# Moving the expert-weight preparation out of the attention loop of a fused patch-embed, attention and mixture-of-experts kernel

## The reference, cut to what matters

```python
h = concatenate([tok(x), txt], axis=1)                # [32, 164, 192]
h = h + attn(layernorm(h))                            # keys, values, gate of batch 0 alone
# attn: fw = 0.95*fw + 0.1*g0*(k0 outer v0); retrieved = q @ fw; x + retrieved @ w_out.T
h = h + ffn(layernorm(h))
# ffn: xn = rms_norm(x); probs = softmax(xn @ router_w.T); top 2 of 8 experts
#      y = sum over the two of probs[e] * (silu(xn @ gate_w[e].T) * (xn @ up_w[e].T)) @ down_w[e].T
#      result y + x
```

## Time and profile before

| what | us |
|---|---|
| median of three runs | 677.99 |
| the profiled execution, its own time | 683.48 |
| its span, first to last instruction | 681.7 |
| PE busy in the span | 543.7 |
| DVE busy | 406.0 |
| ACT busy | 300.6 |
| POOL busy | 198.3 |

### The profile page before, as it was taken

How to read it: one execution, slowest core, us unless ns; L and a number is a source line. 1 busy time by engine, 2 the same in 40 slices (tenths; PEclk the granted TensorE clock), 3 DMA queues, 4 the chain that set the end, 5 groups by cost and what they waited for, 6 DMA issues and landing times.

```text
span 681.7 us, 13237 instructions
## 1 busy us (share of the span) xinstructions
PE 543.7 (80%) x3330; PEld 504.9 (74%) x3331; DVE 406.0 (60%) x1343; ACT 300.6 (44%) x696; POOL 198.3 (29%) x293
## 2 busy tenths in 40 slices
PE   0079989997699999997019999999999999999300
PEld 0067688997497788886019999999999999999300
DVE  4590717666314789999715656565665656565297
ACT  0035991223523677876314444444544444444100
POOL 0001510000000267777702333333333333333300
PEclk9999997999579999998559999999999999999855
DMA  9999600000951022222222322222222222222398
GB/s 201 236 173 187 120 0 1 7 1 0 225 159 36 22 73 74 82 78 81 78 77 52 82 68 80 69 80 69 69 80 72 77 68 81 68 80 61 107 373 259
DMA packets 85235, 64.87 MB, mean 95 GB/s; under 512 B 42500, under 2 KB 81896, under 8 KB 84824
## 3 DMA queue, kind: packets, MB, share of 16 engines
q1 hardware_dynamic: 67160, 39.93, 26.4%
q0 software_dynamic: 8208, 16.95, 6.9%
q10 hardware_dynamic: 9840, 7.67, 3.9%
HBM read 42.61 MB, written 21.86 MB: 95 GB/s over the span
## 4 chain that ended last, share of the span: by engine, by line
PE 65%; DVE 15%; ACT 8%; DMA 6%; issue 3%; SPq 2%; ACTq 1%; POOL 0%; POOLq 0%; DVEq 0%
PE pair L736 9%; PE bank L931 5%; PE bank L927 5%; PE bank L928 4%; PE bank L930 4%; PE bank L929 4%; PE bank L938 4%; DVE hres L1334 4%; ACT sqjunk L463 4%; PE pair L947 4%; PE bank L947 4%; DMA bet<-in_L_tok_ln_beta 3%; PE pair L916 3%; PE pair L806 3%; PE bank L687 3%
## 5 line engine op out<-in xcount | busy, mean ns | idle before, releaser
L648 POOL DMA_INDIRECT disp<-xf,posu x82 | 79.7, 972 | 166.6 <-DVE posu L1212 142.0
L660 POOL DMA_INDIRECT ydram<-ysb,dnow x89 | 87.3, 981 | 69.4 <-POOL dnow L657 67.1
L1310 DVE TENSOR_TENSOR hh<-sg,bank 128x384 f32<-128x384 f32 x89 | 49.3, 554 | 84.0 <-ACT sg L601 84.0
L601 ACT ACTIVATE sg<-bank 128x384 f32<-128x384 f32 x89 | 43.7, 491 | 110.9 <-PE bank L931 110.9
L736 PE MATMUL pair<-wcT,imgT 128*128 128x193 f32 x432 | 74.7, 335 | 3.3 <-DVE tmp L1048 3.3
L736 PEld LDWEIGHTS pair<-wcT,imgT 128*128 128x128 f32 x432 | 73.7, 196 | 3.5 <-issue 3.5
L927 PE MATMUL bank<-wa,xh 128*128 x178 | 67.5, 379 | 0.0
L931 PE MATMUL bank<-wa,xl 128*128 x178 | 60.0, 337 | 0.0
L928 PE MATMUL bank<-wa,xh 128*128 x178 | 60.0, 337 | 0.0
L929 PE MATMUL bank<-wa,xl 128*128 x178 | 59.8, 336 | 0.0
L930 PE MATMUL bank<-wa,xh 128*128 x178 | 59.7, 335 | 0.0
(11 more groups left out here) (229 smaller groups left out, 1258.0 us busy)
## 6 DMA issues: line engine op xcount, KB each, us to landing
xs<-disp SPq DMA_DIRECT2D x89, 96.0 KB, 2.0
img<-in_x SPq DMA_DIRECT2D x12, 392.0 KB, 8.3
yall<-ydram SPq DMA_DIRECT2D x5, 768.0 KB, 13.9
yall<-ydram ACTq DMA_DIRECT2D x5, 768.0 KB, 15.0
hres<-in_txt SPq DMA_DIRECT2D x4, 768.0 KB, 13.2
xs<-disp SPq DMA_DIRECT2D x89, 33.5 KB, 1.9
wraw<-in_L_tok_W SPq DMA_DIRECT2D x1, 2880.0 KB, 17.0
raw_gu<-in_L_ffn_gate_w SPq DMA_DIRECT2D x7, 288.0 KB, 10.7
```

Source lines behind the costliest of these rows:

```text
L648: pool.indirect_dma_start(disp, bass.IndirectOffsetOnAxis(ap=posu[c % XBUF][:, 2 * j + k:2 * j + k + 1], axis=0), xfd[c % XBUF][:, j, :], None
L660: pool.indirect_dma_start(ydram, bass.IndirectOffsetOnAxis(ap=dnow[b][:], axis=0), ysb[b][:], None).then_inc(s_ys[b], 16)
L1310: v.tensor_tensor(hh[o][:], sg[o][:], bank[2 * o + 1][:, 0:DE], ALU.mult).then_inc(s_hh, 1)
```

## The change

All weight units leave the attention loop and run behind it, over four banks (2, 3, 0, 1) instead of two. On PE units 0 to 3 stand right behind the last chunk, ahead of the last ranks and of the counts, and the other 40 behind the counts. On ACT all 44 stand behind the last `add_norm2`. On DVE all 44 stand behind the table.

In a chunk, PE now takes the ranks of the chunk before right after the first `past`, and goes tile by tile. DVE takes `picks(c)` ahead of `stats_2(c)` and `mask(c+1)`, and `places(c)` in the same chunk, ahead of `scale2(c)`; the row numbers are written by one instruction instead of two, and the two small copies into `xf` move from DVE to ACT, into `norm2`. SP's fills wait for the counts (`s_cnt`) alone, not for the table, and the fill that needs no count goes first. The exponentials and weights move behind the expert loop: on DVE behind its last slot, on ACT behind its loads of `yall`.

```diff
@@ -333,6 +332,13 @@
             k = n - NE * FC // 2
             return None if k < 0 else (k // 4, k // 2 % 2, k % 2)
 
+        def unit_bank(n):
+            return (2, 3, 0, 1)[n % 4]
+
+        def unit_done(n):
+
+            return max((k + 1 for k in range(n) if unit_bank(k) == unit_bank(n)), default=0)
+
         def load_results(eng, t):
 
             n = min(GROUP, TILES - t)
@@ -384,12 +390,13 @@
             for which, w in enumerate((gate_w, up_w)):
                 sp.dma_start(raw_last[:, which], w[NE - 1].rearrange("(c f) d -> f c d", f=P)).then_inc(s_raw7, 16)
 
-            sp.wait_ge(s_tab, 1)
+            sp.dma_start(disp[NE * REGION:NE * REGION + P, :], zrow[:]).then_inc(s_zf, 16)
+            sp.wait_ge(s_cnt, 1)
             for e in range(NE):
                 n = sp.value_load(cti[0:1, 1, e:e + 1], min_val=0, max_val=TILES * P)
                 sp.dma_start(disp[bass.ds(n + e * REGION, P), :], zrow[:]).then_inc(s_zf, 16)
-            sp.dma_start(disp[NE * REGION:NE * REGION + P, :], zrow[:]).then_inc(s_zf, 16)
             sp.wait_ge(s_zf, 16 * (NE + 1))
+            sp.wait_ge(s_tab, 1)
 
             for p in range(XBUF):
                 for j in range(4):
@@ -540,9 +547,14 @@
 
             def norm2(c):
                 act.wait_ge(s_s2, c + 1)
-                for j in range(nt(c)):
-                    if c >= XBUF:
-                        act.wait_ge(s_scat[c % XBUF][j], scattered(c))
+                n, x = nt(c), c % XBUF
+                if c >= XBUF:
+                    for j in range(n):
+                        act.wait_ge(s_scat[x][j], scattered(c))
+                nc.scalar.copy(xfd[x][:, 0:n, D + 1:DROW],
+                               cst[:, C_DEST + 4 * c:C_DEST + 4 * c + n].unsqueeze(2).to_broadcast([P, n, 2]))
+                nc.scalar.copy(xfd[x][:, 0:n, D], idxf[:, 8 * c:8 * c + 2 * n].rearrange("p (j k) -> p j k", k=2)[:, :, 0])
+                for j in range(n):
                     nc.scalar.activation(xfd[c % XBUF][:, j, 0:D], hres3[:, 4 * c + j, :], ACT.Identity,
                                          scale=rs[:, c, 1, j:j + 1], bias=bb[:, c, 1, j:j + 1]).then_inc(s_xf, 1)
 
@@ -570,26 +582,22 @@
             for c in range(CHUNKS):
                 if c + 1 < CHUNKS:
                     xT_out(c + 1, 0)
-                high(4 * c)
-                high(4 * c + 1)
                 if c + 1 < CHUNKS and nt(c + 1) > 2:
                     xT_out(c + 1, 1)
                 if c:
                     norm2(c - 1)
                 if c + 1 < CHUNKS:
                     state_out(c + 1)
-                high(4 * c + 2)
                 if c + 2 < CHUNKS:
                     rows(c + 2)
                 if c:
                     add_norm2(c - 1)
                 std2(c)
-                high(4 * c + 3)
             norm2(CHUNKS - 1)
             add_norm2(CHUNKS - 1)
-
-            act.wait_ge(s_w, 1)
-            nc.scalar.activation(top8[:, 0:8 * TILES], top8[:, 0:8 * TILES], ACT.Exp).then_inc(s_exp, 1)
+            for n in range(UNITS):
+                high(n)
+
 
             def step(k, b, parts="xsht"):
 
@@ -614,6 +622,8 @@
                 act.wait_ge(s_ys[b], 16 * ((SLOTS + 1 - b) // 2))
             for g in range(GROUP, TILES, 2 * GROUP):
                 load_results(act, g)
+            act.wait_ge(s_w, 1)
+            nc.scalar.activation(top8[:, 0:8 * TILES], top8[:, 0:8 * TILES], ACT.Exp).then_inc(s_exp, 1)
             store_results(act, 1)
 
         @block.gpsimd
@@ -829,9 +839,9 @@
                 if n == NE * FC // 2:
                     pe.wait_ge(s_rawg, 16 * 2 * (NE - 1))
                     pe.wait_ge(s_raw7, 32)
-                if n >= 2:
-                    pe.wait_ge(s_lo, n - 1)
-                b = bank[2 + n % 2]
+                if unit_done(n):
+                    pe.wait_ge(s_lo, unit_done(n))
+                b = bank[unit_bank(n)]
                 if unit(n) is None:
                     for kk in range(2):
                         e, c = (2 * n + kk) // FC, (2 * n + kk) % FC
@@ -853,7 +863,6 @@
             for c in range(CHUNKS):
                 if c + 1 < CHUNKS:
                     turn(c + 1, 0)
-                expert(4 * c)
                 pe.wait_ge(s_ns, c + 1)
                 pe.wait_ge(s_rows, 2 * c + 2)
                 if c:
@@ -861,40 +870,39 @@
                 if c >= 2:
                     pe.wait_ge(s_pos, c - 1)
                 past(c, 0)
-                if nt(c) > 2:
-                    past(c, 2)
+                if c:
+                    ranks(c - 1)
                 pe.wait_ge(s_sm, c + 1)
                 last = present(c, 0)
                 if nt(c) > 2:
-                    present(c, 2)
-                else:
-                    last.then_inc(s_o, 1)
-                expert(4 * c + 1)
+                    past(c, 1)
+                    last = present(c, 1)
+                last.then_inc(s_o, 1)
                 if c + 1 < CHUNKS and nt(c + 1) > 2:
                     turn(c + 1, 1)
                 if nt(c) > 2:
-                    past(c, 1)
-                    present(c, 1).then_inc(s_o, 1)
                     if c:
-                        ranks(c - 1)
+                        pe.wait_ge(s_pos, c)
+                    past(c, 2)
+                    present(c, 2)
                     past(c, 3)
                     present(c, 3).then_inc(s_o, 1)
-                else:
-                    ranks(c - 1)
                 if c + 1 < CHUNKS:
                     state(c)
-                expert(4 * c + 2)
                 if c + 2 < CHUNKS:
                     rows(c + 2)
                 if c + 1 < CHUNKS:
                     scores(c + 1)
-                expert(4 * c + 3)
-
+
+            for n in range(4):
+                expert(n)
             pe.wait_ge(s_pos, CHUNKS - 1)
             ranks(CHUNKS - 1)
             pe.wait_ge(s_pos, CHUNKS)
             pe.matmul(bank[6][:, RK + 64:RK + 64 + NE], onesb[:], ecs[:, :, nt(CHUNKS - 1)], start=True, stop=True
                       ).then_inc(s_cread, 1)
+            for n in range(4, UNITS):
+                expert(n)
 
             pe.wait_ge(s_lo, UNITS)
             pe.wait_ge(s_tab, 1)
@@ -1201,15 +1209,11 @@
                                         bank[6][:, RK:RK + NE * n].rearrange("p (e j) -> p j e", e=NE).unsqueeze(2)
                                         .to_broadcast([P, n, 2, NE]), ALU.mult))
                 st.link(v.tensor_reduce(rk, ohm[:, 0:16 * n].rearrange("p (a e) -> p a e", e=NE), AX.X, ALU.add))
-                st.link(v.scalar_tensor_tensor(out=posf[:, 0:2 * n], in0=fi, scalar=float(REGION), in1=rk,
-                                               op0=ALU.mult, op1=ALU.add))
                 if c >= XBUF:
                     for j in range(n):
                         v.wait_ge(s_scat[x][j], scattered(c))
-                st.mark(v.tensor_copy(xfd[x][:, 0:n, D + 1:DROW],
-                                      cst[:, C_DEST + 4 * c:C_DEST + 4 * c + n].unsqueeze(2).to_broadcast([P, n, 2])))
-                st.mark(v.tensor_copy(xfd[x][:, 0:n, D], fi.rearrange("p (j k) -> p j k", k=2)[:, :, 0]))
-                v.tensor_copy(posu[x][:, 0:2 * n], posf[:, 0:2 * n]).then_inc(s_pos, 1)
+                v.scalar_tensor_tensor(out=posu[x][:, 0:2 * n], in0=fi, scalar=float(REGION), in1=rk,
+                                       op0=ALU.mult, op1=ALU.add).then_inc(s_pos, 1)
 
             def scale2(c):
                 n = nt(c)
@@ -1236,31 +1240,22 @@
                 ins.then_inc(s_lo, 1)
 
             mask(0)
-            low(0)
-            low(1)
             for c in range(CHUNKS):
                 residual(c)
                 sums(c)
-                if c:
-                    places(c - 1)
+                picks(c)
                 stats_2(c)
-                low(4 * c + 2)
                 if c + 1 < CHUNKS:
                     mask(c + 1)
-                low(4 * c + 3)
-                picks(c)
-                if c + 1 < CHUNKS:
-                    low(4 * c + 4)
+                places(c)
                 scale2(c)
-                if c + 1 < CHUNKS:
-                    low(4 * c + 5)
-            places(CHUNKS - 1)
 
             v.wait_ge(s_cread, 1)
             cnt, til, cum, fst, one = (ct[:, k, :] for k in range(5))
             st.mark(v.memset(one, 1.0))
             st.mark(v.tensor_scalar(cnt, bank[6][:, RK + 64:RK + 64 + NE], float(P - 1), None, ALU.add))
-            st.link(v.tensor_copy(cti[:, 1, :], bank[6][:, RK + 64:RK + 64 + NE]))
+            v.tensor_copy(cti[:, 1, :], bank[6][:, RK + 64:RK + 64 + NE]).then_inc(s_cnt, 1)
+            st.wait()
             st.link(v.tensor_copy(cti[:, 0, :], cnt))
             st.link(v.tensor_scalar(cti[:, 0, :], cti[:, 0, :], 7, None, ALU.arith_shift_right))
             st.link(v.tensor_copy(til, cti[:, 0, :]))
@@ -1282,16 +1277,8 @@
             v.tensor_copy(tab[:, 1, :], slotf[:, 0, :]).then_inc(s_tab, 1)
```

(33 more changed lines are left out.)

## The result

The changed kernel takes 691.41 us, the median of 4 runs (690.08 to 691.75), against 678.20 for the kernel before (4 runs, 677.66 to 678.62): a ratio of 1.0192 [1.0174, 1.0209], 13.2 us slower. The forecast was 682.0, with a range of 675.5 to 690. The sign was right; the loss is three times the forecast.

A forecast was written before the change was run, and what follows sets the result against it. Bounds named: DVE and POOL at 10.2 us a chunk in the attention loop, SP's fills and loads between loops, DVE at the end. Front -0.6 plus softmax +4.6 gave +4.0 on 677.99: 682.0, range 675.5 to 690.

The forecast's parts named there:

- step 4: Units in one piece behind the table: eight down units 8.8 us, 32 gate and up units 18.7, expert loop at 353.9.
- gain of the front: 0.6 us: Up to the expert loop's start: weight work in the open eats the savings, leaving 0.6 us gained.
- Step 1: Attention loop without units: PE waits for DVE's mask behind `picks`; 9.9 us a chunk instead of 10.2.
- The rival of the faster loop: Attention loop: PE's own work sets the pace, some 8.5 us a chunk, total 675; chance 0.15.
- Step 2: Last chunk: units 0 to 3, last ranks and ACT's norms lead to counts at 318.0, 13.5 us earlier.
- Ranks hidden behind ACT's norms: Last chunk: the ranks cost nothing while ACT's norms cover them, up to 2 us without that cover.
- Step 3: Table 6.8 us, fills done some 12.5 us after the counts, first loads landing near 336; nothing waits for them.
- Its remark on what is next: Between the loops: were the units gone, the scatters would be the next limit.
- The rival of the slow clock: Unit stretch: PE stays at 1.2 GHz, giving 687.7 in all, or 691 with down units at 1.74; chance 0.2.
- if the units end ... after 358: Unit stretch: the prediction counts as wrong if the units end before 350 or after 358.
- Step 5: End of the kernel: exponentials wait behind ACT's load issues, so DVE's sum starts at 653.4, 4.6 us lost.
- Softmax hidden: End of the kernel: the exponentials get past the blocked load issues, 677.4, no change; chance 0.1.
- The new wait in the loop: Attention loop: `norm2` with its two copies on ACT delays the next chunk's `past`, 685 to 687; chance 0.1.

The follow-up runs named there:

- the mended kernel: Changed kernel with mask ahead of picks, exponentials ahead of ACT's loads, down units' transposes ordered by form: ratio 0.9976 on a stalling chip; 677.26 us, ratio 0.9982 on another.
- the kernel with PE kept busy: Changed kernel with 24 unused fp32 matmuls of 128 columns added on PE behind the counts, while DVE makes the table: 690.27 us, ratio 1.0167.

## Why the prediction was wrong in size

The sum was "-0.6 + 4.6 = +4.0". By t it measures 155.07 - 146.56 = +8.51 for the front, 10.97 - 6.54 = +4.43 for the softmax, and +0.53 for three stretches around it (the expert loop, its last `ysb` to the loads, and the sum itself, each below 0.2): 13.5. Against the second profile of the kernel before, the front is 155.07 - 145.89 = +9.2, so its size is known to about 1 us. So **step 4's "gain of the front: 0.6 us" is what failed**. It measured a loss of 8.5. The mechanism was the one forecast, down to who releases the first slot; its terms were mis-sized, and all on the same side.

**Step 1** held in its mechanism: PE waits for the mask, 15.1 us in ten waits, and moving `picks` takes that wait away. Chunk 0's last `present` came at t = 8.0 (8.15 forecast), the first scatter and the last one where they were said to be. What it had wrong was the kernel before: "two engines thus sit at one pace" names DVE and POOL, but PE was busy for 100.16 of 102.00 us there, against DVE's 77.98. The new loop was worked out from its own chain, so the forecast didn't suffer by it. The last `present` of chunk 9 came at 302.05 - 202.38 = 99.7 instead of 97.25. About 1.3 of it is the pace, 10.0 to 10.1 instead of 9.9 over nine chunks, and 1.3 is the last chunk's, in which the masks are 307.80 - 296.43 = 11.4 us apart: PE's clock was at 0.75 there (296 to 300 us, PE busy 2.86 of 4.00), and from the mask to the last `present` it took 5.62 us instead of 4.39. The forecast had no term for that. The rival of the faster loop is refuted at 10.1.

**Step 2** had the counts at 318.0, 13.5 us earlier; they came 10.7 earlier. The loop's 2.4 is nearly all of it. Units 0 to 3 ran at 0.52 and took 5.6 us, inside the 3.5 to 7.0 of the text. The ranks behind them, at 314.43, came last: DVE waited 2.52 us for them, and ACT, which was said to cover this, had ended its roots at 313.38. "Ranks hidden behind ACT's norms" was wrong by 1.0 us: from the end of the roots to the counts it took 2.3 us, where 318.0 - 316.5 = 1.5 was forecast.

**Step 3** held: table 6.8 us, fills 9.07 us, nobody waits for a load. Its remark on what is next held as well: in the mended kernel the fills have landed at 323.9 and the last scatter at 329.4, and the loads go out at 330.5.

**Step 4**, by its terms. Counts and table were late by 2.8 us already. The eight down units took 1.40 each, 11.2 instead of 8.8, with the clock at 0.50 throughout (+2.4). The gate and up units took (356.49 - 335.86) / 32 = 0.645 each for either form, 20.6 us instead of 18.7 (+1.9): DVE's low parts back to back are not the mean of 0.53 and 0.64. Both were starts of another, smaller instruction behind a low part. Handovers, from the table to PE and from the last down unit to DVE's first gate unit, took 0.6 more than forecast, and PE began the expert loop 357.45 - 356.49 = 0.96 behind the last low part, for which the sum had nothing. 2.8 + 2.4 + 1.9 + 0.6 + 0.96 = 8.7, from 146.4 to 155.1. The "about 0.4" for a warm start didn't come either: PE was idle for 2.97 us ahead of the first slot and met it at 0.51.

The rival of the slow clock was half true. It named 687.7; its down units at 1.3 were nearer than my 1.1, but PE was no bound for the gate and up units, where the clock came to 1.00 by 340. The bounds of the stage, 349 to 364, held what was measured, 155.07 + 207.55 = 362.6 by the start of before's profile. The range of the total didn't: the terms were taken at middle values, and all went the same way. The sign "if the units end ... after 358" was met: they ended at t = 154.1, which is 361.7 by that profile's start. The upper end of the stage with the softmax's 4.6 on top would have been 677.99 + 9.9 + 4.6 = 692.5, and that far end I had left out.

**Step 5** held: 4.4 where 4.6 was forecast; 4.7 came back when the exponentials went first, and moving the softmax alone cost 4.3 by the ratio. "Softmax hidden" is refuted.

**The new wait in the loop**, on ACT, was not seen: of all of PE's waits from 202 to 309 us, one of 0.2 us ahead of `past` is for ACT's `nst`, in the last chunk.

## What to carry to other kernels

Taking work out of a loop shortens the loop only as far as the next wait, and the work costs its full time where it is put instead, unless something longer runs there anyway: here the table came 10.8 us earlier, and from there to the expert loop it is 35.0 us instead of 15.7. Before a stretch of small transposes is priced, take it at the lower clock and at the rate of the same instruction back to back, not at a gap to another one; and add up the unfavourable bounds of terms that share a cause, as one case. Nothing that others wait for belongs behind the issue of large loads on the same queue; and of the two parts of this change that were run alone, the wait narrowed to what it needs was the one that paid, 6 to 8 us.

## What the hardware showed

**Order of the transposes.** At the same granted clock of 0.50, a 128-row transpose followed by a 64-row one costs 0.70 us a pair, and two of each in a row cost 1.02 for two pairs. Each change of form costs: the next weight load, which otherwise starts under the running transpose, starts only with its own (see the rows of PEld above). Why it does so the traces don't show.

**The clock under transposes.** With PE busy without a gap, the clock fell from 1.00 to 0.50 under alternating transposes (328.2 us in the kernel with PE kept busy), and in the changed kernel it rose from 0.50 to 1.00 between 336 and 344 us, with only transposes on PE since the counts, and only those of the gate and up units, all of 128 rows, from 334.30 on. The Trainium skill, TensorE: Matmul & The Clock Gate, Part 4, says that the fast clock doesn't engage for transposes. The first of these stretches agrees, the second doesn't, and the measurement decides: transposes alone can bring the clock up. When they do stays open. With the down units ordered by form, not alternating, it stayed at 0.50 too, from 324 to 332 us with PE busy throughout; and with two banks it stayed at 0.50 under the 128-row transposes alone, with PE busy for 24.66 of 33.70 us.

**Loads held up at the issue.** Five 768 KB loads held ACT's queue for 7.8 to 8.1 us in every trace. Where the table load and the exponentials stood behind them, these waited.

**Small DVE instructions.** The copy of 128x8 in `picks` had a median of 0.25 us in the kernel before (0.18 in its second profile), 0.37 in the changed one and 0.17 with the mask ahead of the picks, at the same shape. It goes with POOL's scatters: of the 140 such copies in the fourteen traces 35 took 0.32 us or more, and every one of these starts 0.52 to 0.62 us after the start of a scatter. In the changed kernel one takes 0.38 at 241.77, with a scatter since 241.20; with the exponentials ahead of the loads one takes 0.18 at 254.97, with the next scatter at 255.03. Chunks follow it: in the changed kernel and in the one with the exponentials first they are 9.82 us long where this copy takes 0.18 and 10.1 where it takes 0.33 or more, beside the 9.9 of the forecast, but for the chunks in which the clock falls. That the scatter is the cause is inferred from these times; no run here moved it alone.

**The stages ahead**, the same code in all these kernels, took between 202.3 and 207.6 us in their profiles. A stage compared from the span's start can carry all of that.
